# Two graph layers on one core: the stretch between the layers and the end in six chunks, with loads, factors and a node table moved

## What is computed

```python
edge_index = jnp.stack([src, dst])
# layer 0: h = tanh([x[src'], x[dst']] @ W0 + b0); h = tanh(h @ W1 + b1); h = h @ W2 + b2
#          h = h * (edge_attr @ Wg); mean over the edges of one node
x = _layernorm(x + _L0_gnn_ref(x, edge_attr_128, src, dst, W0, b0, W1, b1, W2, b2, Wg), axis=-1)
# layer 1: h = x @ W (4 heads of 64); e = leaky(a_src.h[src] + a_dst.h[dst]) * edge_weight
#          alpha = exp(e - max) / (sum over a node's edges + 1e-10); out = sum(alpha * h[src])
x = _layernorm(x + _L1_gnn_ref(x, edge_index, edge_weight, W, a_src, a_dst), axis=-1)
return x
```

## Time and profile before

| | us |
|---|---|
| median of 3 runs (2465.61 to 2472.03) | 2468.64 |
| the profiled execution | 2466.78 |
| its span | 2465.0 |
| first layer, whose group loop runs from about 110 to 1600 | 0 to 1636 |
| between the layers, to the first gather of HT's rows at 1695.59 | 1636 to 1696 |
| second layer | 1696 to 2401 |
| end | 2401 to 2465 |

### The profile page before, as it was taken

One profiled execution on the slowest core, in us unless ns is written; L12 is line 12 of the kernel. 1 busy time (PEld: TensorE's weight loads), 2 busy tenths in 40 slices (PEclk: granted clock), 3 DMA queues, 4 the chain that ended last, 5 costly groups with the idle time before them and its releaser, 6 DMA issues.

```text
span 2465.0 us, 41568 instructions
## 1 busy us (share of the span) xinstructions
PE 1989.2 (81%) x12990; PEld 1757.5 (71%) x12990; DVE 1594.8 (65%) x4240; ACT 1416.0 (57%) x2926; POOL 1473.5 (60%) x1204
## 2 busy tenths in 40 slices
PE   7799999999999999999999999945155655555560
PEld 6699889999999999989999989943144444444450
DVE  6466666666666666666666666654266566666575
ACT  2488888888888888888888888834011111111112
POOL 0327777777776777767777777423555555555503
PEclk9899999999999999999999999977567767776785
DMA  6888877777777777777777777574344544444413
GB/s 209 282 208 184 193 165 164 167 163 170 159 158 155 161 158 158 159 157 160 158 160 158 160 159 156 112 186 126 91 113 121 128 112 118 119 119 115 120 48 108
DMA packets 236177, 370.91 MB, mean 150 GB/s; under 512 B 35853, under 2 KB 168935, under 8 KB 235949
## 3 DMA queue, kind: packets, MB, share of 16 engines
q0 software_dynamic: 101232, 188.20, 38.7%
q1 hardware_dynamic: 134717, 179.94, 24.7%
HBM read 270.57 MB, written 97.45 MB: 149 GB/s over the span
## 4 chain that ended last, share of the span: by engine, by line
PE 56%; issue 18%; DVE 11%; ACT 5%; DMA 5%; another core or an unknown queue 4%; POOL 1%; SPq 0%; DVEq 0%; ACTq 0%; POOLq 0%
PE bank L1412 12%; PE bank L1410 12%; PE bank L1411 12%; PE bank L1462 4%; PE bank L1453 4%; DMA accA<-ystage,to_a 3%; PE bank L1479 2%; DVE in_window L860 2%; PE bank L1503 2%; PE bank L1514 2%; PE bank L1504 2%; PE bank L1515 2%; PE bank L1578 1%; ACT drop L1849 1%
## 5 line engine op out<-in xcount | busy, mean ns | idle before, releaser
L1306 POOL DMA_INDIRECT accA<-ystage,to_a x391 | 649.7, 1662 | 233.8 <-issue 111.6
L1312 POOL DMA_INDIRECT GA<-TA,src_c x391 | 426.7, 1091 | 323.3 <-issue 95.4
L1341 POOL DMA_INDIRECT Hg<-HT,src_c x391 | 372.9, 954 | 335.6 <-DVE xb L912 174.8
L1849 ACT ACTIVATE drop<-neg_m 128x1 f32<-128x1 f32 x98 | 28.9, 295 | 613.1 <-issue 348.2
L1410 PE MATMUL bank<-h1h,W1h 128*128 128x512 f32 x882 | 349.2, 396 | 1.5 <-DVE h1l L536 1.4
L1412 PE MATMUL bank<-h1h,W1l 128*128 128x512 f32 x882 | 348.3, 395 | 0.0
L1411 PE MATMUL bank<-h1l,W1h 128*128 128x512 f32 x882 | 347.3, 394 | 0.0
L536 DVE TENSOR_TENSOR h2l<-h2f,h2h 128x512 fp32r<-128x512 f32 (+1 forms) x294 | 202.9, 690 | 202.6 <-issue 78.9
L1607 PE MATMUL bank<-diag,ones 128*128 128x128 f32 x196 | 66.5, 435 | 306.3 <-DVE diag L896 250.2
L1617 PE MATMUL bank<-xb,in_window 128*128 128x260 f32 (+1 forms) x782 | 292.9, 542 | 1.1 <-issue 1.1
L536 DVE TENSOR_TENSOR h1l<-h1f,h1h 128x512 fp32r<-128x512 f32 x294 | 195.1, 691 | 131.3 <-ACT h1h L1686 114.2
(11 more groups left out here) (208 smaller groups left out, 5196.0 us busy)
## 6 DMA issues: line engine op xcount, KB each, us to landing
TW<-TB SPq DMA_DIRECT2D x196, 203.0 KB
ef<-in_eT SPq DMA_DIRECT2D x97, 256.0 KB
bcast_i<-in_src_row SPq DMA_DIRECT2D x97, 256.0 KB
HB<-hist SPq DMA_DIRECT2D x98, 130.0 KB
rel<-RL SPq DMA_DIRECT2D x97, 128.0 KB
rem<-RD SPq DMA_DIRECT2D x48, 256.0 KB
TB<-stB SPq DMA_DIRECT2D x24, 406.0 KB
accA<-zeros SPq DMA_DIRECT2D x4, 1677.0 KB, 13.1
```

The source lines that it names most:

```text
L1306: return pool.indirect_dma_start(out=table, out_offset=bass.IndirectOffsetOnAxis(ap=rows, axis=0), in_=sums, in_offset=None, compute_op=AL ...
L1312: pool.indirect_dma_start(out=GA[0:n, b % (GAR * BLOCKS_PER_GROUP), :].bitcast(f32), out_offset=None, in_=TA, in_offset=bass.IndirectOffse ...
L1341: pool.indirect_dma_start(out=Hg[0:n, slot, :], out_offset=None, in_=HT, in_offset=bass.IndirectOffsetOnAxis(ap=src_c[0:n, b:b + 1], axis= ...
```

## The change

The chunks are now six: tiles 0 to 2, then four of five tiles, then tiles 23 and 24. `norm_factors(c - 1)` moves into chunk c: between the layers behind the add of its tables, at the end behind the weighing of its rows. A third table buffer is there. WcT and ablk are loaded in the first layer behind group 14's loads (nine transfers), and ablk is cleared ahead of that layer's loop; Wc gets a counter of its own. ACT takes one square root of a constant (`warm`) and copies the eight columns of Wc ahead of the wait for the last sums; `deviations(c+1)` moves behind two thirds of chunk c's tiles, and at the end behind `normalise(c)`. PE issues twenty products of the identity that nobody reads when the first tables have landed. The store of DT goes; `hst` holds all 264 columns, and POOL copies the four of `node` out of it. DVE's window arithmetic moves ahead of the wait for the sums.

```diff
+    CHUNKS = [range(a, b) for a, b in zip((0, 3, 8, 13, 18, 23), (3, 8, 13, 18, 23, NT))]
+    NC = len(CHUNKS)
+    TC = max(len(tiles) for tiles in CHUNKS)
-        TSR = 2
+        TSR = 3
-        hst = sb("hst", [P, 4, BW], f32, s1)
+        hst = sb("hst", [P, 4, BW + HEADS], f32, s1)
@@ vector, mean_residual(c)
                 dve.tensor_tensor(rows[:, 0], rows[:, 0], rows[:, 1], ALU.add).then_inc(s_sum, 1)
+                if c >= 1:
+                    norm_factors(c - 1, c - 1)
@@ vector, attention_residual(c)
                 last.then_inc(s_att, 1)
+                if c >= 1:
+                    norm_factors(c - 1, NC + c - 1)
@@ vector, between the layers (the window arithmetic now stands ahead of this)
+            wait_stage_a(dve)
+            const(dve.memset(node[:, :, :], 0.0), "node clear")
+            dve.wait_ge(s_xn, 48)
+            for c in range(NC):
+                mean_residual(c)
+            norm_factors(NC - 1, NC - 1)
+
             dve.wait_ge(s_hc, NT)
+            dve.wait_ge(s_nd, NT)
@@ sync
+                if g == 14:
+                    sp.wait_ge(s_dc, DC["ablk"])
+                    sp.dma_start(WcT[:, :, :], WcatT.rearrange("(k p) n -> p k n", p=P)).then_inc(s_ldc, 16)
+                    for h in range(HEADS):
+                        k, r = divmod(h * HD, P)
+                        sp.dma_start(ablk[r:r + HD, k, h:h + 1], a_src[h, :, :]).then_inc(s_ldc, 16)
+                        sp.dma_start(ablk[r:r + HD, k, HEADS + h:HEADS + h + 1], a_dst[h, :, :]).then_inc(s_ldc, 16)
@@ sync, between the layers
             load_tables(sp, range(TSR))
+            sp.dma_start(Wc[:, :, 0:OUT], Wcat.rearrange("(k p) n -> p k n", p=P)).then_inc(s_ldWc, 16)
+            load_tables(sp, range(TSR, 5))
+            for c in range(NC):
+                for t in tiles_of_chunk(c):
+                    n = rows_of_tile(t)
+                    sp.wait_ge(s_hc, t + 1)
+                    for r, e in pieces(t):
+                        sp.dma_start(HT[t * P + r:t * P + e, :], hst[r:e, t % 4, 0:BW]).then_inc(s_ht[t % 4], 16)
+                load_tables(sp, range(c + 5, min(c + 6, NC)))
-            sp.dma_start(DT[0:full * P, :].rearrange("(t p) h -> p t h", p=P), node[:, 0:full, :]).then_inc(s_st, 16)
-            sp.dma_start(DT[full * P:N, :], node[0:N - full * P, full, :]).then_inc(s_st, 16)
@@ gpsimd, ahead of the gathers of HT's rows
+            pool.wait_ge(s_dc, DC["node clear"])
+            for t in range(NT):
+                n = rows_of_tile(t)
+                pool.wait_ge(s_hc, t + 1)
+                pool.tensor_copy(node[0:n, t, :], hst[0:n, t % 4, BW:BW + HEADS]).then_inc(s_nd, 1)
+            pool.wait_ge(s_nd, NT)
@@ tensor (the wait for s_wac moves into node_products(0), with one for s_ldWc)
+            pe.wait_ge(s_tab[0], chunk_arrivals(0))
+            for _ in range(20):
+                pe.matmul(bank[3][:, 0:P], ident[:, :], ident[:, :], start=True, stop=True)
@@ scalar
-            copy(node[0:n, t, :], bank[t % 4][0:n, BW:BW + HEADS])
-            copy(hst[0:n, t % 4, :], bank[t % 4][0:n, 0:BW]).then_inc(s_hc, 1)
+                act.wait_ge(s_nd, t - 3)
+            copy(hst[0:n, t % 4, :], bank[t % 4][0:n, 0:BW + HEADS]).then_inc(s_hc, 1)
+            act.activation(warm[:, :], eps[:, :], ACT.Sqrt)
             act.wait_ge(s_wa, 1)
@@ scalar, between the layers
-                if t % TC == 0:
-                    if t // TC + 1 < NC:
-                        deviations(t // TC + 1, t // TC + 1)
-                    normalise(t // TC, t // TC)
+                for c, tiles in enumerate(CHUNKS):
+                    if t == tiles[0]:
+                        normalise(c, c)
+                    if t == tiles[2 * len(tiles) // 3] and c + 1 < NC:
+                        deviations(c + 1, c + 1)
@@ scalar, end
+            deviations(0, NC)
             for c in range(NC):
-                deviations(c, NC + c)
-                if c >= 1:
-                    normalise(c - 1, NC + c - 1)
-            normalise(NC - 1, 2 * NC - 1)
+                normalise(c, NC + c)
+                if c + 1 < NC:
+                    deviations(c + 1, NC + c + 1)
```

More of the change, by code:

```diff
@@ L210, in build_program @@
         eq_low = sb("eq_low", [P, 2, P], bf16, sa)
+        WcT = sb("WcT", [P, DK, OUT], f32, sa)
+        ablk = sb("ablk", [P, DK, 2 * HEADS], f32, sa)
         sa.close()
@@ L257, in build_program @@
         x1T = sb("x1T", [P, XTR, DK, P], f32, s1)
-        WcT = sb("WcT", [P, DK, OUT], f32, s1)
-        ablk = sb("ablk", [P, DK, 2 * HEADS], f32, s1)
-        hst = sb("hst", [P, 4, BW], f32, s1)
+        hst = sb("hst", [P, 4, BW + HEADS], f32, s1)
         s1.close()
@@ L490, in tiles_of_chunk @@
         def tiles_of_chunk(c):
-            return range(c * TC, min((c + 1) * TC, NT))
+            return CHUNKS[c]
         def load_tables(eng, chunks):
@@ L722, in _ @@
             const(dve.memset(ml[:, :, :, OUT:AW].bitcast(f32), 0.0), "ones")
+            const(dve.memset(ablk[:, :, :], 0.0), "ablk")
             for s in range(-2, NG + 1):
@@ L793, in norm_factors @@
                     .then_inc(s_shift, 1)
-            wait_stage_a(dve)
-            const(dve.memset(ablk[:, :, :], 0.0), "ablk")
-            const(dve.memset(node[:, :, :], 0.0), "node clear")
-            dve.wait_ge(s_xn, 48)
-            for c in range(NC):
-                mean_residual(c)
-                if c >= 1:
-                    norm_factors(c - 1, c - 1)
-            norm_factors(NC - 1, NC - 1)
+            dve.wait_ge(s_Yc, NB)
             low = low_all[:, 0, :]
@@ L1402, in _ @@
                     out=fin[:, t, :], out_offset=None, in_=HB,
-                    in_offset=bass.IndirectOffsetOnAxis(ap=row_i[:, t:t + 1], axis=0)).then_inc(s_fin[t // TC], 16)
+                    in_offset=bass.IndirectOffsetOnAxis(ap=row_i[:, t:t + 1], axis=0)).then_inc(s_fin[[t in tiles for tiles in CHUNKS].index(True)], 16)
         @block.tensor
```

37 lines of the change are left out of this document (9 added, 28 removed).

## The result

The changed kernel takes 2462.19 us (median of 20 runs, 2454.01 to 2470.96) against 2469.44 for the kernel before in the same comparison. The ratio is 0.9968, with a 95% interval of 0.9957 to 0.9978: **7.9 us faster (5.4 to 10.6)**. The forecast was 14.3 us faster. The second comparison, on another chip, gave 0.9970 (0.9958 to 0.9981), again some 7.5 us.

The account below looks back on a forecast made before the run. Bounds: waits between the layers, a 70 us crawl beside POOL's gathers, and the end. Boundary 7.7, store 3.0 and end 3.6 sum to 14.3 us: 2468.64 to 2454.3, range 2443 to 2463.

Parts of the forecast that it names:

- Start of the boundary: Between the layers: first normalisation at about 1647.3 instead of 1655.3, the next at 1653.4.
- Rest of the boundary: Between the layers: four chunks at 6.7 us, the last 5.7, end at 1685.9; whole boundary gains 7.7 us.
- unread products: Twenty TensorE products between the layers, ended by 1650.8; taken as 0, ends -1 and +1.
- Wc: Between the layers: lands about 1649.5, before 1653.4; rival: products wait for it, gain 4 not 7.7, 2458.0, chance 0.12.
- Store of DT: Start of second layer: without the store remainders land earlier; 3.0 us gained, between 0 and 6.2.
- the crawl: Second layer's first 70 us, no engine busy but POOL sending gathers; maxima 29 us apart; its end may ignore DVE's start.
- The rival that the crawl absorbs the early start: Start of second layer: the same number of groups is through at the crawl's end; 2457.3, chance 0.20.
- End: Last chunks of the second layer: tail falls from 7.5 to 3.9 us, gain 3.6, ends 0 and 11.1.
- slow stretch: DVE's third chunk at the end, 7.5 us lost, assumed to stay; rival that it goes: 2446.8, chance 0.13.
- POOL's copies: 25 small copies between the layers, taken as 0; rival that they hold DVE: 2471.3, chance 0.05.
- Moved loads: Nine DMAs at group 14 of the first layer, 5.5 us of SP's queue, hidden; ends 0 and +2.
- Second layer's loop: 84 groups behind the crawl, 568 us, 6.8 each, held to be unchanged.

Follow-up runs that it names:

- e1: The changed kernel run again, nothing altered, on another chip: 2454.04 us against 2462.33 for the kernel before, ratio 0.9970.
- e3: The changed kernel with the old end (five chunks of five tiles, old order of ACT's work): 2454.83 us, ratio 0.9965 to the kernel before.
- e4: The changed kernel with POOL allowed four groups of gathers ahead of DVE instead of twelve: 2424.85 us, ratio 0.9856 to the kernel before.
- e11: The changed kernel, POOL four groups ahead, with Wc loaded behind the first pair of tables instead of the third: ratio 0.9842 to the kernel before.
- e12b: The changed kernel with POOL pausing every second group, plus one pause at the end and fourteen more unread products: 2384.48 us, ratio 0.9667 to the kernel before.
- e2: The kernel before without the store of DT and the waits for it: ratio 1.0004 to the kernel before.
- e8: The changed kernel, POOL four groups ahead and waiting before every group until the one before has landed: 2516.58 us, ratio 1.0204 to the kernel before.
- e9: The changed kernel, twelve groups ahead, POOL waiting before every second group until the one before has landed: 2391.01 us, ratio 0.9717 to the kernel before.
- e10: The changed kernel with four chained clears on POOL (1.01 us) before every second group, instead of a wait for landing: 2454.61 us, ratio 0.9976 to the kernel before.

## Why the forecast was right in its sign and nearly twice too large

14.3 us were forecast and 7.9 measured (5.4 to 10.6). Two of the three terms of the sum came to nothing, and 2462.19 lies only 0.8 us inside the stated range of 2443 to 2463, so that it lies inside owes something to luck.

- **Start of the boundary: right.** First and second normalisation came 10.2 and 16.3 us behind the request, 10.7 and 16.8 in the working. The table load and the product of WcT and ablk are off the path.
- **Rest of the boundary: the rate was right, one chunk was not.** 7.7 us were forecast, 6.5 were found in the first trace, 5.4 to 6.5 over e1, e3 and e4 (57.1 less 51.7 to 50.6; nine traces with the new boundary lie between 50.5 and 52.0, three with the old one between 56.7 and 57.8). The step that was mis-sized is the rate of 6.7 us taken for chunk 1 too, with the unread products put at 0 as a raised clock only shortens tiles that wait for ACT anyway. In chunk 1 ACT waits for PE: the clock was raised, then lost in the gaps in front of it, and the chunk took 1.5 to 2.7 us more. e11 and e12b show it from both sides. No run leaves the twenty products out, so their own worth is not measured.
- **Wc: the wait was there, as the rival said, but for chunk 0's products only** (until 14.5 us behind the request; the landing was forecast at 12.9). It did not delay the next normalisation, which came as reckoned, but it is one of the two gaps in which the clock was lost.
- **Store of DT: 3.0 us forecast, 0 found** (e2: 1.0004). The one-hot did come earlier, 5.1 us behind the last copy of h instead of 11.6. The step that failed is that one more group may be through by the end of the crawl. The rival that the crawl absorbs the early start was right in its mechanism, and the distance of 78.1 us between the first gather and the third maximum held to 0.8 us in all traces with twelve ahead and no pause.
- **End: 3.6 us forecast, 0 found** (e3). I had priced the slow stretch as a constant 7.5 us. It is a stretch of fixed place behind POOL's first gather, and what it costs depends on how many tiles are done when it ends. So the moments were not ready as early as before, but 2.5 us later behind the first gather. The tail was mis-sized too, 4.9 us for 3.9: ACT is still normalising the five tiles of chunk 4 (until 2448.59) when the last moments are there at 2447.52, and the last root waits for it.
- **POOL's copies: 0 forecast, 0 found.** The copies wait for DVE instead. The working called the issue of 0.95 us the nearest row; the trace before has small operations on POOL at its start, such as an iota of 128x1 with 0.13 us, and a copy took 0.19. **Moved loads: 0 forecast;** the group loop of the first layer shows no difference above its own variation.
- **Second layer's loop: forecast unchanged; not settled** (e1). If it did change, it was by a few us.

Of the boundary's gain 0.5 us is lost again ahead of the first gather, which comes 2.5 us behind the last copy of h instead of 2.0; I did not look for the reason. What the runs show of the boundary adds up to 4.9 to 5.9 us of the 7.9 measured (5.4 to 10.6), so no further cause is needed, and none is excluded; a loop shorter by some 2 us would fit.

## What to carry to other kernels

An early start is worth something only if what follows is not timed by something else: look for the next stretch in which no engine is busy, and ask which engine's work it begins and ends with. Where GpSimd sends many gathers without a stop, try a pause of two idle microseconds per eight of them; with this and nothing else this kernel gained a further 62 us (ratio 0.9717 against 0.9970; 50 to 75 by the intervals), eight times what the whole change did, while a pause per four gathers lost more than it gave (e8). And look at the clock where the products that count begin, not where the unread ones end: here gaps of 1.79 and 1.36 us between the two were followed by a clock of 0.50, and with the gaps filled it stayed at 1.00 (e12b).

## What was not expected of the hardware

The loop of the changed kernel, two groups:

```profile
2004.89 0.79 PE L1624 MATMUL bank<-diag,ones 128*128 128x128 f32 x2 [5.00 <-DVE diag L904]
2005.79 0.28 DVE L911 TENSOR_REDUCE top_g<-bank 128x1 f32<-128x128 f32 x1
...
2009.92 0.79 PE L1624 MATMUL bank<-diag,ones 128*128 128x128 f32 x2 [0.47 <-DVE top_c L899]
...
2012.28 0.95 POOL L1346 DMA_INDIRECT Hg<-HT,src_c  x1 [0.30 <-issue]
2013.27 0.29 DVE L911 TENSOR_REDUCE top_g<-bank 128x1 f32<-128x128 f32 x1 [2.37 <-remote]
```

- While GpSimd sends gathers back to back, TensorE's results and, at the end, VectorE's instructions come late. In the rows above DVE takes the maximum 0.90 us after PE's products start, and one group later 3.35 us after, 0.04 us behind the end of the eighth gather (2013.23). At the end the late stretch begins 21 us after the first gather. In the changed kernel's loop held maxima come 0.0 to 1.7 us behind the end of POOL's last gather, 0.37 in the mean; in the crawl the third comes 8.5 us behind it (1761.21 and 1769.75). An idle POOL of 2.0 to 2.7 us per eight gathers avoids the crawl (e9); a break of 1.28 us, 1.01 of it filled with clears, does not (e10). The time in between was not tried.
- The cause of that is open. It is not that DVE waits for gathered rows, since it waited for PE there. Nor does the release need all gathers landed: in e9 the maximum comes 1.29 us behind the end of the last gather of the run, and POOL's wait for that gather's group ends 1.37 us later (1709.00). It is not VectorE's program, as the stretch at the end kept its place behind POOL's first gather when the chunks moved. The Trainium skill (Runtime: NRT & Kernel Launch, "Instruction fetch mechanics") says that each engine's sequencer fetches its instructions by its own transfers while it runs. Between 1700 and 1770 the changed kernel's trace holds no packet of an instruction queue, where the 100 us before hold eight. That would fit starved sequencers, but as well engines that made no progress and so had nothing to fetch. In the loop 30 such packets come in 500 us, one in 17, while the holds come each 13 us, so I do not call it shown.
- The 5.0 us of one group and the 7.5 to 8.4 of the next, through nearly the whole second layer, are tied to POOL: eight gathers of 1.254 us, and some 3 us in which the held results pass and release the ring. Behind the last gather every group takes 5.0.
